# Layer 1 cross-attention scores in a two-layer decoder: high and low f32r parts stacked on four groups of 32 rows

## What is computed

```python
Q = _split_heads(x @ Wq.T + bq, N_HEADS)                  # (2, 16, 512, 8)
K = _split_heads(knowledge_embeddings @ Wk.T + bk, N_HEADS)  # (2, 16, 77, 8)
V = _split_heads(knowledge_embeddings @ Wv.T + bv, N_HEADS)
scores = jnp.einsum('bhsd,bhnd->bhsn', Q, K) / SCALE
topk_scores, topk_indices = jax.lax.top_k(scores, k)      # k = 32
sparse_weights = jax.nn.softmax(topk_scores, axis=-1)
```

## Time and profile before

| | |
|---|---|
| time, median of 3 runs | 606.18 us (605.25 to 607.37) |
| span of the profiled execution | 618.7 us |
| PE busy | 545.9 us, 88% |
| DVE busy | 396.9 us, 64% |
| ACT busy | 303.2 us, 49% |
| POOL busy | 223.6 us, 36% |
| mean granted TensorE clock | 0.959 |

### The profile page before, as it was taken

One profiled execution on the slowest core, in us unless ns is written; L12 is line 12 of the kernel. 1 busy time (PEld: TensorE's weight loads), 2 busy tenths in 40 slices (PEclk: granted clock), 3 DMA queues, 4 the chain that ended last, 5 costly groups with the idle time before them and its releaser, 6 DMA issues.

```text
span 618.7 us, 12164 instructions
## 1 busy us (share of the span) xinstructions
PE 545.9 (88%) x3982; PEld 426.4 (69%) x3982; DVE 396.9 (64%) x2193; ACT 303.2 (49%) x758; POOL 223.6 (36%) x227
## 2 busy tenths in 40 slices
PE   4889779997899899989999879888699899979997
PEld 2565337874667566768677657677477778979997
DVE  3565765534433598776598998956757898744543
ACT  2342314325775676674874646635574555322221
POOL 4016830002434464563553556541614334340000
PEclk9996889999999999998988999968889999999999
DMA  4500102404000000000000000003500000010000
GB/s 129 179 1 14 40 25 68 124 30 154 3 1 1 0 2 1 3 1 2 2 2 1 2 2 1 2 2 102 179 22 10 14 15 19 18 31 1 27 1 10
DMA packets 23050, 19.17 MB, mean 31 GB/s; under 512 B 2048, under 2 KB 18508, under 8 KB 22989
## 3 DMA queue, kind: packets, MB, share of 16 engines
q1 hardware_dynamic: 22477, 17.36, 9.2%
q0 software_dynamic: 512, 1.05, 0.6%
HBM read 15.38 MB, written 3.01 MB: 30 GB/s over the span
## 4 chain that ended last, share of the span: by engine, by line
PE 65%; DVE 20%; ACT 8%; issue 4%; another core or an unknown queue 1%; POOL 1%; DMA 0%; DVEq 0%; ACTq 0%
PE ps L1797 54%; DVE wk L1159 4%; PE ps L2187 4%; DVE top L1149 3%; DVE nmax L1101 2%; ACT w_mem L1549 2%; PE ps L2249 2%; ACT prT L1562 2%; DVE sel_mem L994 1%; PE ps L2382 1%; DVE xn L1122 1%; PE ps L2441 1%; PE ps L1809 1%; DVE xn L838 1%
## 5 line engine op out<-in xcount | busy, mean ns | idle before, releaser
L1101 DVE TENSOR_REDUCE nmax<-ps 128x2 f32<-128x256 f32 (+1 forms) x64 | 51.2, 821 | 63.9 <-PE ps L1797 62.0
L1159 DVE MATCH_REPLACE8 wk<-top,wk 128x77 f32<-128x77 f32 x384 | 80.5, 223 | 0.9 <-issue 0.9
L687 POOL TENSOR_TENSOR w_mem<-w_mem,rinv 128x256 f32<-128x256 f32 (+3 forms) x44 | 53.2, 1219 | 53.9 <-DVE rinv L1107 53.4
L1280 DVE TENSOR_TENSOR sel_mem<-gr,ps 128x512 f32<-128x512 f32 x47 | 32.2, 685 | 53.4 <-ACT gr L1739 52.7
L1149 DVE MAX8 top<-wk 128x8 f32<-128x77 f32 x384 | 58.2, 223 | 1.9 <-DVE top L1149 1.8
L1739 ACT ACTIVATE gr<-ps 128x512 f32<-128x512 f32 x47 | 28.1, 598 | 62.2 <-PE ps L1797 62.2
L1797 PE MATMUL ps<-cat_mem 64*128 64x512 f32 (+7 forms) x272 | 54.0, 477 | 1.5 <-ACT cat_mem L1533 1.5
L716 POOL TENSOR_SCALAR wk<-wk 128x616 f32<-128x616 f32 x16 | 28.1, 1755 | 60.6 <-DVEq L1163 60.3
L1549 ACT ACTIVATE w_mem<-ps,nmax 128x128 f32<-128x128 f32 (+3 forms) x88 | 44.4, 519 | 11.1 <-DVE nmax L1101 10.9
L1797 PE MATMUL ps<-prT,cat_mem 128*64 128x128 f32 x640 | 45.5, 293 | 1.4 <-DVE x L1184 0.9
L611 POOL TENSOR_TENSOR rstd<-var_eps,minus_half 128x4 f32<-128x4 f32 x8 | 8.2, 1025 | 97.8 <-DVE var_eps L831 97.7
(11 more groups left out here) (346 smaller groups left out, 1372.8 us busy)
## 6 DMA issues: line engine op xcount, KB each, us to landing
w_mem<-in_L_ffn_W_dram SPq DMA_DIRECT2D x12, 256.0 KB, 3.1
f_mem<-in_L_ffn_Wg_dram SPq DMA_DIRECT2D x8, 256.0 KB, 2.7
f_mem<-in_L_ffn_Wu_dram SPq DMA_DIRECT2D x8, 256.0 KB, 3.1
f_mem<-in_L_ffn_Wd_dram SPq DMA_DIRECT2D x8, 256.0 KB, 4.1
sel_mem<-in_L_ffn_W_dram SPq DMA_DIRECT2D x4, 256.0 KB, 4.8
xs_dram<-zero SPq DMA_DIRECT2D x1, 960.0 KB, 6.3
ys_dram<-f_mem SPq DMA_DIRECT2D x15, 64.0 KB, 1.5
xs<-xs_dram SPq DMA_DIRECT2D x3, 256.0 KB, 4.7
```

Of the source, the lines that this page charges most:

```text
L687: pool.tensor_tensor(pr[s][:, :, at:at + n], pr[s][:, :, at:at + n], rinv[:, i % 8, :].unsqueeze(2).to_broadcast([P, 2, n]), ALU.mult)\
L1101: dve.tensor_reduce(nmax[:, i % 8, :], ps[:, 2 * s:2 * s + 2, at:at + (c + 1) * P], X, ALU.max, negate=True).then_inc(nmax_ready, 1)
L1159: dve.match_replace(wk[q][:, t, h, :], top[q][:, t, h, 8 * r:8 * r + 8], src[:, t, h, :], GONE).then_inc(top_step, 1)
L1280: dve.tensor_tensor(hg[s][:, :], gr[s][:, :], ps[:, 2 * s + 1, :], ALU.mult)\
```

## The change

Keys and queries of one group of four heads have 32 rows. The changed kernel stacks four copies of these 32 rows on the 128 partitions: high, low, high, low parts of the keys (`kc_parts`, `ks`) against high, high, low, low parts of the queries (`qs`). One f32r matmul over all 128 rows then gives all four products, so `scores_x` is one f32r pass.

For that the weights of queries and keys are written four times per group (`wq4`, `wk4`; the former lies in the buffer `gr[0]`, which is free until the experts). A query projection now gives one group, so a block needs four matmuls of 128 x 256 and not one, in two halves of two. `QUERIES` says at which step a half stands. ACT copies each group rounded to f32r, and DVE subtracts that from PSUM plus bias on partitions 64 to 127 for the low part (`queries_low`). The keys take four matmuls, four copies on ACT, and on POOL a cast, two subtractions on 32 partitions, and four masked copies of 128 x 616 in place of 16 of 128 x 154. The wait on `kc_ready` or `qc_ready` before scores becomes one on `kc_qlo_ready`, which DVE raises last. Two DMAs of a bias of 1 x 128 become DMAs of 4 x 4 x 32. `cnT` moves into rows of `bias_rows` that are free by then.

```diff
+QUERIES = {11: (0, 0), 14: (0, 1), 27: (1, 0), 30: (1, 1), 36: (2, 0), 37: (2, 1)}
...
-        kh = sb("kh", [P, B, HX, NC])
+        ks = sb("ks", [P, 4, B, 4, NC], f32r)
...
-        qc = sb("qc", [P, S])
+        qs = sb("qs", [P, 4, 2 * P], f32r)
...
-            pool.wait_ge(kc_ready, 1)
-            for h in range(HX):
-                pool.tensor_scalar(kh[:, :, h, :], kc[:, :, :], head_mask[:, h:h + 1], None, ALU.mult)
+            pool.wait_ge(kc_qlo_ready, 4)
+            pool.tensor_copy(kc_parts[:, :, :], kc4[:, :, :]).then_inc(pool_step, own.up())
+            pool.wait_ge(pool_step, own.now())
+            for r in (32, 96):
+                rows = slice(r, r + 32)
+                pool.tensor_tensor(kc_parts[rows, :, :], kc4[rows, :, :], kc_parts[rows, :, :].bitcast(f32), ALU.subtract)\
+                    .then_inc(pool_step, own.up())
+            pool.wait_ge(pool_step, own.now())
+            for h in range(4):
+                pool.tensor_scalar(ks[:, :, :, h, :].rearrange("p g b n -> p (g b) n"),
...
+            def queries_low(k, half, bank):
+                dve.wait_ge(qc_ready, 4 * k + 2 * half + 2)
+                for g in (2 * half, 2 * half + 1):
+                    dve.scalar_tensor_tensor(qs[DH:P, g, :], ps[DH:P, bank, 2 * P * (g % 2):2 * P * (g % 2 + 1)],
+                                             vec[DH:P, VEC["x1_bq"] + g:VEC["x1_bq"] + g + 1],
+                                             qs[DH:P, g, :].bitcast(f32), ALU.add, ALU.subtract).then_inc(kc_qlo_ready, 1)
...
+                if U in QUERIES:
+                    queries_low(*QUERIES[U], 7)
...
+                if b in (4, 6):
+                    queries_low(3, b // 2 - 2, 4)
...
             act.wait_ge(cross_ps, 1)
-            act.activation(w_x1T[:, :, :], tiles(2), ACT.Copy).then_inc(x1T_ready, 1)
+            act.activation(w_x1T[:, :, :], tiles(2)[:, 2:4, :], ACT.Copy).then_inc(x1T_ready, 1)
+            for k, w4 in enumerate((wq4, wk4)):
...
-            def evac_qc(k, source):
-                act.wait_ge(qc_ps, k + 1)
-                act.activation(qc[:, 2 * P * (k % 2):2 * P * (k % 2 + 1)], source, ACT.Identity, bias=bias("x1_bq"))\
-                   .then_inc(qc_ready, 1)
+            def evac_qc(k, half, bank):
+                act.wait_ge(qc_ps, 2 * k + half + 1)
+                for g in (2 * half, 2 * half + 1):
+                    act.activation(qs[:, g, :], ps[:, bank, 2 * P * (g % 2):2 * P * (g % 2 + 1)], ACT.Identity,
+                                   bias=bias("x1_bq", g)).then_inc(qc_ready, 1)
...
-            def queries(k, out_q, *free):
+            def queries(k, half, bank, *free):
                 for signal, count in free:
                     pe.wait_ge(signal, count)
                 pe.wait_ge(qnT_ready, k + 1)
-                mm(out_q, w_x1T[:, 0, :], block_tokens(k)).then_inc(qc_ps, 1)
-                return ((qc_ready, k + 1),)
+                for g in (2 * half, 2 * half + 1):
+                    last = mm(ps[:, bank, 2 * P * (g % 2):2 * P * (g % 2 + 1)], group4(0, g), block_tokens(k))
+                last.then_inc(qc_ps, 1)
+                return ((kc_qlo_ready, 4 + 4 * k + 2 * half + 2),)
...
-                pe.wait_ge(qc_ready, k + 1)
-                at = 2 * P * (k % 2) + t * P
-                mm(ps[:, bank, 0:4 * NC], qc[:, at:at + P], kh[:, k // 2, 4 * (n % 4):4 * (n % 4) + 4, :])\
-                    .then_inc(half_ps, 1)
+                pe.wait_ge(kc_qlo_ready, 4 + n + 1)
+                mm(ps[:, bank, 0:4 * NC], qs[:, n % 4, t * P:(t + 1) * P],
+                   ks[:, n % 4, k // 2, :, :].rearrange("p h n -> p (h n)")).then_inc(half_ps, 1)
...
-                if b == 3:
-                    four = queries(3, out_x, *four)
+                if b in (3, 5):
+                    four = queries(3, b // 2 - 1, 4, *four)
```

More of the change, by code:

```diff
@@ L358, in decoder @@
         gr = [sb(f"gr{s}", [P, S]) for s in range(2)]
+        wq4 = part(gr[0], 0, 4, 4, 32)
         hg = [sel_mem[:, (4 + s) * S:(5 + s) * S] for s in range(2)]
@@ L463, in decoder @@
         w_x1 = sb_begin("w_x1", [P, 4, D])
-        kc = sb_begin("kc", [P, B, NC])
+        wk4_mem = sb_begin("wk4", [P, 4 * P])
+        wk4 = part(wk4_mem, 0, 4, 4, 32)
+        kc4 = sb_begin("kc4", [P, 4, B * NC])
+        kc_parts = sb_begin("kc_parts", [P, 4, B * NC], f32r)
         wr = sb_begin("wr", [E, D])
@@ L652, in _ @@
                 rstd_of(n)
-            pool.wait_ge(kc_ready, 1)
-            for h in range(HX):
-                pool.tensor_scalar(kh[:, :, h, :], kc[:, :, :], head_mask[:, h:h + 1], None, ALU.mult)
+            for n in (8, 4):
+                pool.tensor_tensor(head_mask[:, 0:n], head_mask[:, 0:n], head_mask[:, n:2 * n], ALU.add)\
+                    .then_inc(pool_step, own.up())
[6 more added lines that the diff above has]
+                pool.tensor_tensor(kc_parts[rows, :, :], kc4[rows, :, :], kc_parts[rows, :, :].bitcast(f32), ALU.subtract)\
+                    .then_inc(pool_step, own.up())
+            pool.wait_ge(pool_step, own.now())
+            for h in range(4):
+                pool.tensor_scalar(ks[:, :, :, h, :].rearrange("p g b n -> p (g b) n"),
+                                   kc_parts[:, :, :].bitcast(f32).rearrange("p g (b n) -> p (g b) n", b=B),
+                                   head_mask[:, h:h + 1], None, ALU.mult).then_inc(pool_step, own.up())
             for b in range(B):
@@ L1467, in _ @@
             act.wait_ge(cross_ps, 2)
-            act.activation(wrT[:, :], ps[:, 0, 2 * P:2 * P + E], ACT.Copy)
-            act.activation(kc[:, :, :], ps[:, 0, 0:B * NC].rearrange("p (b n) -> p b n", b=B), ACT.Identity,
-                           bias=bias("x1_bk")).then_inc(kc_ready, 1)
+            act.activation(wrT[:, :], ps[:, 0, 3 * B * NC:3 * B * NC + E], ACT.Copy)
+            for g in range(3):
+                act.activation(kc4[:, g, :], ps[:, 0, g * B * NC:(g + 1) * B * NC], ACT.Identity,
+                               bias=bias("x1_bk", g)).then_inc(kc_qlo_ready, 1)
             evac_qx(1)
@@ L1475, in _ @@
             act.wait_ge(cross_ps, 3)
+            act.activation(kc4[:, 3, :], ps[:, 1, 2 * P:2 * P + B * NC], ACT.Identity, bias=bias("x1_bk", 3))\
+               .then_inc(kc_qlo_ready, 1)
             act.wait_ge(const_xlo_ready, 2)
@@ L1632, in _ @@
                         evac_v(j, 6)
-                for k in range(3):
-                    if U == STAGE[k + 1] + 3:
-                        evac_qc(k, spare)
+                if U in QUERIES:
+                    evac_qc(*QUERIES[U], 7)
                 if U == 12:
@@ L1754, in _ @@
                     norm_two(3, qnT_ps, qnT_ready, four)
-                if b == 3:
-                    evac_qc(3, four)
+                if b in (3, 5):
+                    evac_qc(3, b // 2 - 1, 4)
                 if b == 7:
@@ L1945, in queries0, with group4 @@
                 mm(ps[:, b, :], w_x0q[:, 0, :], tokens(b)).then_inc(qx_ps, 1)
+            def group4(k, g):
+                return (wq4, wk4)[k][:, g, :, :].rearrange("p c r -> p (c r)")
             def keys():
                 pe.wait_ge(in_x1, 16 * 7)
-                pe.wait_ge(x1T_ready, 1)
+                pe.wait_ge(x1T_ready, 3)
                 pe.wait_ge(qx_ready, 1)
-                pe.transpose(ps[:, 0, 2 * P:2 * P + E], wr[:, :], ident[0:E, 0:E])
-                mm(ps[:, 0, 0:B * NC], w_x1T[:, 1, :], ctxT[:, :, :]).then_inc(cross_ps, 1)
+                pe.transpose(ps[:, 0, 3 * B * NC:3 * B * NC + E], wr[:, :], ident[0:E, 0:E])
+                for g in range(3):
+                    last = mm(ps[:, 0, g * B * NC:(g + 1) * B * NC], group4(1, g), ctxT[:, :, :])
+                last.then_inc(cross_ps, 1)
             def values_x():
                 pe.wait_ge(qx_ready, 2)
+                mm(ps[:, 1, 2 * P:2 * P + B * NC], group4(1, 3), ctxT[:, :, :])
                 for b in range(B):
                     vo = ps[0:NC, 1, b * D:(b + 1) * D]
-                    mm(vo, ctxT[:, b, :], w_x1T[:, 2, :], stop=False)
+                    mm(vo, ctxT[:, b, :], w_x1T[:, 0, :], stop=False)
                     last = mm(vo, ones[0:1, 0:NC], bias_row("x1_bv"), start=False)
@@ L1996, in _ @@
             values_x()
-            pe.wait_ge(kc_ready, 1)
+            pe.wait_ge(kc_qlo_ready, 3)
             weights_T(0, W_BANKS[0])
@@ L2279, in project_context @@
                 for t in range(2):
-                    last = mm(out_c[:, t * P:(t + 1) * P], tile(cnT, t), w_x1T[:, 3, :])
+                    last = mm(out_c[:, t * P:(t + 1) * P], tile(cnT, t), w_x1T[:, 1, :])
                 last.then_inc(xo_ps, 1)
@@ L2308, in _ @@
                         taken = j + 1
-                for k in range(3):
-                    if U == STAGE[k + 1] + 3:
-                        seven = queries(k, spare, *seven)
+                if U in QUERIES:
+                    seven = queries(*QUERIES[U], 7, *seven)
                 for j in range(2, 4 * NP, 2):
```

22 lines of the change are left out of this document (13 added, 9 removed).

## The result

The kernel after takes 617.16 us (median of 4), the kernel before 605.71 us (median of 4): ratio 1.0172, 95% interval 1.0136 to 1.0207. It is slower by some 11 us (10.4 by the ratio, 11.5 by the medians). The forecast was 605.9 us with a range to 609.5, so both the forecast and the range are missed. A second measurement of the same kernel (e9) gave 1.0178 (1.0130 to 1.0226).

A forecast was written before the change was run, and what follows sets the result against it. The prediction took PE's own instruction order as the bound in most places (65% of the chain); costs of 9.5 us less gains of 9.8 us gave -0.3 us on 606.18, so 605.9 us, range 602.0 to 609.5 us.

The forecast's parts named there:

- The gain from scores: 22 score matmuls on the chain at 0.39 us give 8.6 us, plus 0.7 at b = 4, less 1.0 for DVE.
- The start: Added key matmuls at 42 us cost 0.35 us, one more before the values at 51.5 us costs 0.5: 0.85 us.
- freed step 35: Attention step that loses its query projection and PE's wait for ACT's copy: 1.5 us gained.
- costed at nothing: GpSimd's key cast, subtractions and four longer copies at the start take about as long as its 16 copies: no cost.
- Steps 11 and 14: Block 0's query halves in attention: 0.6 us with DVE's part hidden, and 1.1 us with little DVE slack.
- Step 27: Block 1's first query half in attention: 0.45 us of PE and 0.38 us of ACT's copy, 0.8 us cost.
- Steps 30, 36, 37, b = 4 and b = 5: Later query halves, in attention and before the experts: costs of 1.2, 1.0, 0.85, 1.1 and 2.0 us.
- rival 5: DVE operations starting on partition 64 between others on partition 0 lose overlap: 16 places, 1.3 us, half on chain; 606.6 us, 4%.
- Rival 3: Low part as a link in the PE-DVE-ACT loop, about 2.0 us per half; 610.3 us with six and a half; 17%.
- likeliest case: Gains and added work even out at 605.9 us, 38%; own bounds given as 603.7 to 608.5 us.
- Rival 4: New waits bring PE to half clock in three more places, 4.5 us: 610.4 us; 7%.
- Rival 2: The added work falls into existing waits of DVE and PE, 3.7 us less: 602.2 us; 34%.

The follow-up runs named there:

- e9: The kernel after, unchanged, measured a second time; 1.0178 of before.
- e13: The kernel after's start and f32r scores, but one query matmul and one copy per block at before's places, no low part; 0.9983 of before.
- e4: The kernel before with queries and keys written as f32r and score matmuls in one f32r pass, no low parts; 0.9967 of before.
- e1: The kernel before, unchanged, profiled a second time; ratio 0.9999, span 603.6 us.
- e12: The kernel before with two GpSimd subtractions on scratch added at 54 us, beside DVE's multiplications; second measurement, 1.0057 of before.
- keys late: The kernel after with GpSimd's key preparation moved from 53 us to some 100 us, behind the weight splits; 1.0148 of before.
- e5: The kernel after with GpSimd's key preparation moved from 53 us to some 100 us; 1.0148 of before.
- both moves: The kernel after with keys late and two second halves moved (to step 39 and b = 7); 1.0141, 1.0012 and 1.0129 of before.
- e10: The kernel before with two GpSimd subtractions on scratch added at some 95 us, where DVE isn't waited for; 1.0002 of before.
- e8: The kernel after with both moves, first measurement; 1.0141 of before.
- e18: The kernel after with both moves, third measurement; 1.0129 of before.

## Why the prediction was wrong

Three terms of the sum failed. The gain from scores was 8.3 us in it and 2.1 us when timed alone. The start was 0.85 us and came to about 3. The halves were 8.65 us, less 1.5 for the freed step 35, and came to 11 (after against e13, which keeps step 35 as it was).

**The gain, 9.8 us with step 35: the step that failed most.** The price of a score was right: a pair took 0.79 us, a single record now takes 0.387 us in the mean, so 0.40 us against my 0.39. The count was wrong. I took 22 scores as lying on the chain because PE's piece with them was on it. That reads a chain as if nothing ran just behind it. In the experts' part it was so: six scores, forecast 2.3 us, measured 2.0 us, and the same in every kernel with f32r scores (147.5 to 147.8 us against 149.5 to 149.7). In attention, 14 scores were to give 5.5 us less 1.0. When they alone were changed, the mean stayed at 247.2 us, and at the same time at half clock it fell by about 2. PE's busy time fell all the same and became idle time (before, then e4; stretches with the engines' busy us in the order PE, weight loads, DVE, ACT, POOL, then the granted clock):

```profile
200.00:344.00 144.00, 132.15 (x1099) 99.01 (x1096) 108.16 (x695) 94.57 (x250) 75.04 (x59) 0.98 0.01 2
```

```profile
200.00:344.00 144.00, 128.37 (x1084) 98.40 (x1085) 109.35 (x693) 95.28 (x251) 76.34 (x61) 0.96 0.01 2
```

I had taken off 1.0 us for that. That it was DVE, busy for 108.2 of 144 us, that PE then waited behind is argued from this busy time; no run changes DVE's work alone. The whole gain, timed alone, is 2.1 us (0.3 to 3.9), and some 4 us at the same clock. The 0.7 us added at b = 4 had no ground: PE's wait of 4.08 us and the slow pair behind it belonged to that one execution. In e1 PE doesn't wait there:

```profile
435.08 0.68 PE L1797 MATMUL ps<-kh,qc 128*128 128x308 f32 x2
```

**GpSimd "costed at nothing": wrong.** The cost was sought in its total (11.11 us of copies against as much) and in who waits for its end. Neither moved. It acts through its neighbour: a two-input operation of 1.47 us took DVE's multiplication with it. The start is 3.2 us longer in the mean, 2.6 us at the same time at half clock, against 0.85 forecast for all of it; e12 has 3.4 us. PE's and ACT's added key work, for which the 0.85 us stood, shows as 0.2 to 0.4 us (DVE's same operation at 45.91 and 46.32 us, with 0.25 us of the difference there before the keys). I had used this very effect at step 36, where the profile of before shows it, and didn't look for it at the start. The Trainium skill (SBUF — State Buffer, the section on the two separate sides) says that GpSimd shares one pair of ports with DVE under an exclusive lock. It applies to DVE instructions in a two-port mode or with two inputs in SBUF, and whichever instruction starts first has the pair for its whole length. The long durations here agree (1.64 beside 1.47 us, 1.36 beside 1.21 us in e12); GpSimd's one-input copies of 0.67 us, which stretched 0.34 to 0.43 us only, don't.

**Steps 11 and 14 (1.7 us): nothing in the end.** Both delay DVE's maxima, by 1.3 to 1.5 us, and by 284 us the kernel after is as far behind e1 (4.9 us) as it was at 200 us (4.9 us). Step 27 (0.8 us): 0.3 us.

**Steps 30, 36, 37, b = 4 and b = 5 (6.15 us): about 9.5 us.** After against e1, same operation of DVE behind each: 2.5 us at step 30 (1.3 of it stay), 1.25 at 36, 1.8 at 37, 2.1 at b = 4 and 3.1 at b = 5. These are delays at the place. Between 405 and 419 us after catches up 4 us, since e1 has a granted clock of 0.51 from 405 to 415 us, so that over both stretches this pair of traces differs by 7.4 us. Step 30 in rows (timeline), before and after:

```profile
303.38 0.96 DVE L1101 TENSOR_REDUCE nmax<-ps 128x2 f32<-128x768 f32 x1 [1.25 <-PE ps L1797]
304.25 0.22 DVE L1107 RECIPROCAL rinv<-rsum 128x2 f32<-128x2 f32 x2
304.38 1.20 DVE L1149 MAX8 top<-wk 128x8 f32<-128x77 f32 x8
```

```profile
308.58 0.96 DVE L1121 TENSOR_REDUCE nmax<-ps 128x2 f32<-128x768 f32 x1 [1.20 <-PE ps L1834]
311.13 0.89 DVE L1158 SCALAR_TENSOR_TENSOR qs<-ps,vec,qs 64x256 fp32r<-64x256 f32 x2 [1.47 <-ACT qs L1608]
312.06 1.22 DVE L1176 MAX8 top<-wk 128x8 f32<-128x77 f32 x8
```

1.00 us from maxima to the round became 3.48 us: DVE's wait of 1.47, its work of 0.89, and 0.12 that rival 5 accounts for (below). My "DVE's own delay takes up its 1.26 us" counted idle time that lies ahead of the maxima; the delay lies behind them, and the 1.20 us are still there. At step 37 I priced the work (0.85 us) and let the wait be over, where matmuls, copies and low part are 1.02, 0.84 and 0.89 us in series and PE has nothing else. At b = 6 I looked at what DVE's wait would hold up, and not at PE, whose transposes for piece 10 need bank 4 behind the low part (0.51 us idle, after 0.96 us for the bank ahead of the matmuls). The work of one low part was right (0.45 by the line, 0.488 measured).

**The rivals.** Rival 3, at 17%, was the mechanism: the low part as a link, with 1.25 to 3.1 us per half at five of eight. Its own sum was right for a gain of 9.8, so that it had to reach 5.5 halves to matter; with a gain near 2 it matters from the second half on. That dependence, one gain under all rivals, is also why the range was too narrow. (The likeliest case's own bounds, 1.7 us for the price and 1.0 or 1.2 for step 36, add up to 603.2 to 608.8 us and not to 603.7 to 608.5; nothing hangs on it.)

Rival 4 (the clock), at 7%, came true in part. The median granted clock is 0.9635 in the ten runs of after and 0.972 in the 77 of before, some 10 us more at half clock, and at 0.32 us each that is 3 of the 11 us. Its reason isn't shown. The waits at the halves, which the rival names, can't be all of it, since rounded scores alone bring the clock to 0.964.

Rival 5 shows its sign, but small. In seven of eight halves the operation of DVE behind a low part starts 0.03 us after its end, where neighbours that start on the same partition overlap by 0.08 us: above, the low parts end at 312.02 and `MAX8` begins at 312.06, while before `RECIPROCAL` ends at 304.47 and `MAX8` begins at 304.38. That is 0.12 us a place, 0.8 us of DVE's time in all and less of the kernel's. Two low parts, one behind the other, do overlap (0.89 us for 2 x 0.488). Rival 2 fell.

**What stays open.** How much keys late give back: the starts at the same time at half clock say 1.6 us, timed after to e5 is 1.5 us, and the halves moved to both moves about 1 us. The 3.4 us between e12 and e10 and the 3.2 us between the mean starts hold some clock as well (medians of all runs 0.970 at e12 and 0.972 at e10). Why after and the kernels with rounded scores are granted a lower clock than before is open too, and so is what step 35 gave by itself.

## What to carry to other kernels

Before a shorter operation is priced by its place on the chain, ask which engine ends next there: where another engine is busy three quarters of the stretch, change that operation alone and time it before anything is built around it. Compare granted clocks along with the times, since here a change of 2 us in the time hid one of 4 us in the work. A producer that is made of three engines in series belongs where the consumer has other work and its bank isn't wanted; moving two of eight halves gave 3 to 4 us without taking out an instruction. For each operation that GpSimd gets, look at what DVE does at that moment, not only at who waits for GpSimd.

## What the runs showed of the hardware

- A two-input GpSimd operation of 32 x 616 elements (1.2 to 1.5 us) stretched a DVE multiplication of 0.34 us to 1.36 us in e12 and 1.64 us in after; a one-input GpSimd copy of 128 x 154 elements (0.67 us) stretched it to 0.43 us at most in e1.
- Experts' stretches of kernels with the same kind of scores agree to 0.3 us between executions; the start of one kernel differs by 5.6 us (145.6 and 151.2 us to the first maxima, e8 and e18), with the granted clock 1.00 in one and 0.66 in the other between 45 and 60 us.
- A us at half clock went with 0.32 us of time in 77 runs of before and with 0.30 us in the starts of twenty traces.
- A DVE operation on partitions from 0 on began 0.03 us after a low part on partitions 64 to 127 had ended, in seven places of after; others overlap by 0.08 us.
- One f32r score record of 308 columns took 0.387 us in the mean, a record of the fp32 pair 0.469 us: half the records, but each record's own length hardly tells the saving, which is 0.40 us per score.
